# Moving the output projection's matmuls within the last batch of an attention kernel

## The reference

```python
def _L0_xattn_ref(query, key_value, Wq, bq, Wk, bk, Wv, bv, Wo, bo):
    ...
    scores = jnp.einsum('bhqd,bhkd->bhqk', Q, K) / scale
    weights = jax.nn.softmax(scores, axis=-1)
    attn = jnp.einsum('bhqk,bhkd->bhqd', weights, V)
    attn = attn.transpose(0, 2, 1, 3).reshape(B, SQ, H * Dh)
    return attn @ Wo.T + bo
...
x = x + _L0_xattn_ref(_layernorm(x, axis=-1), ctx_1024, ...)
x = x + _L0_attn_ref(_layernorm(x, axis=-1), ...)
```

## Time and profile before

| | |
|---|---|
| median of 3 runs | 2019.91 us (2019.12 to 2020.32) |
| the profiled execution, its own time | 2021.62 us |
| its span in the trace | 2019.8 us |
| PE busy | 1936.8 us, 96% |
| DVE, POOL, ACT busy | 1424.1 us (71%), 1263.3 us (63%), 895.7 us (44%) |
| last batch, first score maximum to the last shift | 1059.0 to 1182.5 us |
| mean granted PE clock, whole span | 0.983 |

### The profile page before, as it was taken

The page is one execution under the profiler, slowest core; times in us unless marked ns, Lnnn a source line. Parts: engine busy times, 40 slices in busy tenths (PEclk is TensorE's granted clock), DMA queues, the critical chain, the costliest instruction groups (busy, mean ns, idle before and its releaser), DMA issues. The chain is left out here.

```text
span 2019.8 us, 38857 instructions
## 1 busy us (share of the span) xinstructions
PE 1936.8 (96%) x15364; PEld 1416.2 (70%) x15364; DVE 1424.1 (71%) x1479; ACT 895.7 (44%) x1204; POOL 1263.3 (63%) x990
## 2 busy tenths in 40 slices
PE   6989999999999999999998889899999999999998
PEld 5867777777777777777774558555555555768886
DVE  4126777777777777677776856399999998538675
ACT  4124444434444344443433544476676664533340
POOL 4127777777777777777767731089989996325210
PEclk9999999999999999999997899999999999999999
DMA  5546565555555555655544320230040003111201
GB/s 199 158 135 178 157 192 160 177 181 170 183 161 172 168 181 166 181 154 187 175 133 142 111 66 1 51 78 1 1 125 1 1 1 101 42 43 63 92 13 42
DMA packets 180550, 229.31 MB, mean 114 GB/s; under 512 B 21489, under 2 KB 111921, under 8 KB 174225
## 3 DMA queue, kind: packets, MB, share of 16 engines
q1 hardware_dynamic: 180368, 226.82, 36.5%
HBM read 153.18 MB, written 73.56 MB: 112 GB/s over the span
## 5 line engine op out<-in xcount | busy, mean ns | idle before, releaser
L525 POOL TENSOR_TENSOR a_half<-a_pt 128x1024 f32<-128x1024 f32 x128 | 307.6, 2403 | 251.6 <-ACT a_pt L600 243.9
L600 ACT ACTIVATE a_pt<-a_shift 128x2048 f32<-128x2048 f32 x128 | 245.1, 1915 | 471.8 <-PE a_o L903 455.4
L705 DVE TENSOR_TENSOR a_shift<-a_s,a_neg_rows 128x2048 f32<-128x2048 f32 x113 | 259.1, 2293 | 92.4 <-ACT a_neg_rows L611 92.4
L692 DVE TENSOR_REDUCE a_top<-a_s 128x128 f32<-128x2048 f32 x113 | 259.0, 2292 | 40.0 <-PE a_s L860 40.0
L819 PE MATMUL a_pj<-l_x_hi,l_w_hi 128*128 128x512 f32 x448 | 208.0, 464 | 0.0
L516 POOL TENSOR_TENSOR l_x_lo<-a_raw,l_x_hi 128x512 fp32r<-128x512 f32 x120 | 156.1, 1301 | 80.8 <-ACT l_x_hi L587 80.8
L1300 POOL TENSOR_TENSOR s_even_drive<-s_du,l_rows 128x512 f32<-128x512 f32 x128 | 163.0, 1274 | 61.6 <-DMA s_c_row<-bc_scratch 59.8
L1308 POOL TENSOR_TENSOR s_odd_seen<-s_odd_state,s_c_row 128x512 f32<-128x512 f32 x128 | 162.5, 1270 | 34.9 <-DVE s_odd_state L1439 15.2
L1500 PEld LDWEIGHTS s_ps<-s_diag,s_du_t 128*128 128x128 f32 x1024 | 135.8, 194 | 62.3 <-issue 62.3
L821 PE MATMUL a_pj<-l_x_lo,l_w_hi 128*128 128x512 f32 x448 | 177.1, 395 | 0.0
L820 PE MATMUL a_pj<-l_x_hi,l_w_lo 128*128 128x512 f32 x448 | 177.1, 395 | 0.0
(11 more groups left out here) (274 smaller groups left out, 4054.2 us busy)
## 6 DMA issues: line engine op xcount, KB each, us to landing
kv_scratch<-a_k_new SPq DMA_DIRECT2D x128, 256.0 KB, 2.5
kv_scratch<-a_v_new SPq DMA_DIRECT2D x128, 256.0 KB, 3.5
a_stack<-kv_scratch SPq DMA_DIRECT2D x512, 64.0 KB, 2.4
a_v<-kv_scratch SPq DMA_DIRECT2D x32, 1024.0 KB, 6.2
a_raw<-in_ctx SPq DMA_DIRECT2D x120, 256.0 KB, 3.7
a_q_stack<-q_scratch SPq DMA_DIRECT2D x128, 64.0 KB, 2.1
s_c_row<-bc_scratch SPq DMA_DIRECT2D x32, 256.0 KB, 5.8
e_ew_raw<-in_ew SPq DMA_DIRECT2D x8, 1024.0 KB, 4.9
```

Source lines behind the costliest of these rows:

```text
L525: nc.gpsimd.tensor_tensor(half[:], w[:, 0:2], w[:, 2:4], ALU.add).then_inc(halved, 1)
L600: nc.scalar.activation(pt_head(g, p), shift[:].rearrange("p (i n) -> p i n", n=BANK), ACT.Exp).then_inc(exped, 1)
L692: dve.tensor_reduce(top[:], s_ps[:].rearrange("p i n -> p (i n)").rearrange("p (k q) -> p q k", q=L), AX.X, ALU.max).then_inc(blocked, 1)
L705: dve.tensor_tensor(shift[:].rearrange("p (k q) -> p k q", q=L), s_ps[:].rearrange("p i n -> p (i n)").rearrange("p (k q) -> p k q", q=L), ...
```

## The change

In the last batch's loop over heads, on PE alone, the seven-fold sequence of chunks 0 to 3 gets other places. Before, chunk 0 stood behind the weighing of an odd head, chunk 1 between the two turns of the next even head, chunk 2 behind that head's weighing, chunk 3 behind the second turn of the next odd head. Now chunk 0 stands between the turns of an even head, chunk 1 behind its second turn, chunk 2 between the turns of the next odd head and chunk 3 where it was. `turn_normalised` moves from behind the first turn to ahead of it. The number of instructions is the same on every engine; on DVE, ACT, POOL and SP the order is the same too.

```diff
             for h in range(1, H):
                 for s in range(2):
                     half_scores(h, s)
+                turn_normalised(h)
                 turn_half(h, 0)
-                turn_normalised(h)
+                project_output(h, 2, (0,))
+                project_output(h, 3, (2,))
+                turn_half(h, 1)
                 project_output(h, 2, (1,))
-                turn_half(h, 1)
                 project_output(h, 3, (3,))
                 spread_negative(LAST + h, 2)
                 weigh_last(B - 1, h // HG, h % HG, False)
-                project_output(h, 2, (2,))
-                project_output(h, 1, (0,))
```

## The result

| | before | after |
|---|---|---|
| median of 6 runs | 2020.12 us (2019.12 to 2022.2) | 2012.12 us (2011.88 to 2013.31) |
| ratio after / before, 95% interval | | 0.9968 (0.9956 to 0.998) |
| profiled execution: own time, span | 2021.62, 2019.8 us | 2011.88, 2010.1 us |
| first maximum of head 1 to the last head's shift | 121.17 us | 110.70 us |

The change makes the kernel faster, by 8.0 us between the medians. The interval of the ratio puts it between 4 and 9 us. The prediction was 2010.0 us in a range of 2004.5 to 2017.5. The profiled execution of the kernel before lies 1.5 us above its median, so the difference between the two traces (9.7 us of span) is somewhat larger than that between the medians.

The account below looks back on a forecast made before the run. The prediction took DVE to hold most of the pace, idle 17.6 us before next heads' maxima. Terms 3.1 + 6.8 + 1.0 - 1.0 + 0 gave 9.9 us off 2019.9: 2010.0 us, range 2004.5 to 2017.5.

Parts of the forecast that it names:

- the ring: DVE and PE handovers, with an ACT copy, from one head's first maximum to the next; DVE has most of it.
- The sum of 9.9 us: Total of the gains and prices in the last batch, against the profiled execution; taken from the 2019.9 us median.
- head 1 to 2: Scores of head 2 start 3.1 us earlier, without chunk 0 and its wait for DMAs.
- heads 2, 4, 8, 12: Even heads at the low clock lose the chunk behind the weighing: 4 x 1.7 = 6.8 us won.
- heads 6, 10, 14: Even heads at full clock: 0.5 us won before the next maximum, 0.17 paid ahead of the spread; 1.0 us together.
- transposes: turn_normalised ahead of the first turn in heads 7, 9, 11, 13, 15 costs 0.2 us each, 1.0 together.
- heads 3 and 5: Odd heads partly at the low clock: gain 0, bounds -0.85 and +0.9 us each.
- the lower bound of 1.0: Least gain per head in heads 2, 4, 8, 12, priced at the low clock throughout: 2.0 - 1.0 us.
- the price of the two chunks in the turns: In even heads a chunk ahead of the spread costs 0.17 us at full clock, about 1.0 at the low clock.
- The clock is back by the scores: In heads 2, 4, 8, 12 dense work from the first turn restores the clock; another 0.9 us per head goes.
- the clock hardly falls: Rival for the last batch: nearly all DVE waits go and low-clock costs come back, 15.8 us, 2004 us; chance 0.09.
- a sign against it: The low clock in heads 6, 7, 10, 11, 14 or 15 of the profile after would show the prediction wrong.

Follow-up runs that it names:

- the seventh experiment: Changed kernel plus six unread matmuls ahead of the first turn of heads 4, 8 and 12; 2006.53 us, ratio 0.9955 to the kernel before.
- the fifth experiment: Changed kernel with both chunks of heads 4, 8, 12 one place earlier, chunk 0 ahead of the first turn; 2008.72 us, ratio 0.996 to before.
- the third experiment: Changed kernel with chunk 0 left behind the weighing of odd heads and only chunk 1 between an even head's turns; 2015.58 us, ratio 0.9984 to before.
- ninth: Changed kernel plus unread matmuls: six ahead of the first turn of heads 4, 8, 12, three ahead of and three between head 1's turns; 2007.04 us.
- tenth: Kernel with one chunk in even heads plus unread matmuls: three and three in head 1, two behind chunk 0 in heads 4, 8, 12; 2006.92 us.
- eleventh: Changed kernel plus ten transposes of 128x128 ahead of the first turn of heads 4, 8 and 12; 2007.44 us, ratio 0.9951 to before.

## Why the prediction was right

The time came within 2.1 us of 2010.0, and the mechanism, chunks off the ring where DVE waits plus an earlier return of the clock, was the right one. The sum of 9.9 us agrees with the trace's last batch (10.5 us), but by terms that cancel, which is luck. By the table above, before minus after:

| term of the sum | predicted | in the traces |
|---|---|---|
| head 1 to 2 | 3.1 | 3.4 |
| heads 2, 4, 8, 12 | 6.8 | 2.27 + 0.23 + 1.79 + 1.40 = 5.7 |
| heads 6, 10, 14 | 1.0 | 0.19 - 1.05 + 0.16 = -0.7 |
| transposes | -1.0 | 0 to -0.1 |
| heads 3 and 5 | 0 | 0.96 + 1.17 = 2.1 |

**Head 1 to 2.** Right. The weighing ended earlier too, since it had the full clock for part of its time (1.25 against 1.94 us). PE then waited 0.53 us for half 0 of the shift.

**Even heads at the low clock.** The mean was 1.4 instead of 1.7, but head 4 won 0.23 us, far under the lower bound of 1.0. The step that was mis-sized is the price of the two chunks in the turns. The sum took the turns of these heads as at the low clock already. Those of heads 4 and 8 were not:

```profile
1090.29 0.33 PE L879 MATMUL a_m<-l_ident,a_top 128*128 128x128 f32 x1 [1.26 <-DVE a_top L712]
1090.45 1.02 PE L974 MATMUL a_pj<-l_wo,a_v_new 128*128 128x512 f32 x2
...
1092.27 0.32 PE L886 MATMUL a_m<-l_ident,a_neg_max 128*128 128x128 f32 x1 [0.52 <-DVE a_neg_max L718]
```

In head 4 first turn to spread took 1.98 us before and 3.69 us after (1083.01 to 1086.70, shown at the seventh experiment): 1.7 us more, which ate nearly all of the wait of 2.10 us that went. In head 8 it was 2.09 us before and 3.24 us after (1113.16 to 1116.40). "The clock is back by the scores" was right, and saved the term: in all four the scores ran at the full clock, in 2.29 us with the wait for half 1 in them. The fall itself I took as given. It still costs heads 4, 8 and 12 from 1.2 to 1.5 us each: filled, they take 6.60 us instead of 7.83 to 8.14. The case "the clock hardly falls" was priced at 16 us. With the three waits filled the last batch won 121.2 - 108.3 = 12.9, with heads 5 and 13 still falling (3.0 us over 7.11 and 7.13), so its size was about right, but the change alone did not reach it. Its argument that PE's wait would grow from 1.66 to about 2.1 us did not hold: it stayed at 1.66 to 1.67, since PE now waits for the shift ahead of the scores too.

**Full-clock even heads.** Mis-sized from 0.33 to 0.18 each. I let DVE go from the shift straight into the next maximum. In fact shift to next maximum is 2.57 us (1101.01 to 1103.58), with a wait of 0.21 us in every even head: half 0 of the shift, the handover and half of the scores do not quite fit into the shift. And head 10 fell to the low clock, 1.05 us slower than before, which the prediction had named as a sign against it. The stretch ahead of it has no long wait but several short ones: 0.88 us for the shift, a gap between the halves of the scores, 0.47 us for the maximum. PE's chunk behind the weighing had covered the first of them before. But heads 6 and 14 have the same waits (0.89 and 0.47 us) and kept the full clock, so they do not explain the fall by themselves.

**Transposes.** Mis-sized: 0.2 us per head predicted, nothing measured. The first turn comes 0.24 us later, as predicted (1103.58 to 1105.10 is 1.52 instead of 1.28 us), but the second turn waits for the second half's maximum in any case, and the turns move closer (0.97 instead of 1.13 us).

**Heads 3 and 5.** I left their gain at 0 with 0.9 as a bound. Both ran at the full clock after, head 5 in 7.11 instead of 8.28 us. Their 2.1 us hide what the even heads 2, 4, 8, 12 and head 10 won less.

**Behind the last batch** not all moved forward. First mixer matmul minus last head's shift was 1193.83 - 1180.20 = 13.6 us before and 1183.56 - 1169.12 = 14.4 after, and the rest of the kernel took 0.6 us longer. With 0.6 us that the last batch began earlier: 0.6 + 10.5 - 0.8 - 0.6 = 9.7, the difference of the spans.

**What is shown and what is argued.** That the clock at heads 4, 8 and 12 depends on whether PE has something to do ahead of the first turn is shown. In all eight kernels that put something into that place these heads took 6.5 to 6.8 us (only head 8 of the fifth experiment 7.07, with a fall at its end), with work that nobody needs as well as with chunks, and in the kernel before as in the changed one. In the six kernels that leave the place empty the clock fell at 16 of 18 such heads. The two exceptions are heads 8 and 12 of the third experiment, the second with the full wait of 1.66 us. So the wait is what makes a fall likely, and not a sufficient cause of it. Filling does not end all falls: in each of the eight filled kernels at least one of the heads right behind (5, 9 or 13) was at the low clock for a part, and in the changed kernel none of these three was.

That the scatter of the kernel before (10 us) comes from the clock is borne out by its 63 executions beside the experiments: the six fastest, 2011.29 to 2012.80 us, had mean granted clocks of 0.989 to 0.990, and the five above 2021 us 0.982 or 0.983. At which heads those executions fell is not on record, since each kernel has one trace. What decides whether a head with the long wait, or one with only short waits, falls stays open.

## What to carry to other kernels

Read a chain with PE in it at both clock levels before moving anything: at the low one a chunk of matmuls here cost 2.0 us instead of 1.05 and a fitting slot became a delay. Work that PE has to spare belongs where PE waits, and if there is none, a few unread matmuls in a wait of 1.7 us can pay (4.8 us of 2018 here for 18 of them, on the kernel before). Look at the heads behind as well: the fall may come there instead. A handover that waits on a DMA at the entry of a stage is worth its own look: one of 28 chunks carried 3.4 of the 10.5 us, less the 1.3 us that head 2 pays when only that chunk is moved.

## What had not been expected of the hardware

- The kernel before ran between 2011.29 and 2021.82 us in 26 runs; the kernel with the chunks in the turns within 1.4 us in six. The six runs of the kernel before beside those lay within 3.1 us, so that the order changed the scatter is not shown by so few.
- Adding 1.60 us of matmuls in three places made the kernel before faster by 4.8 us.
- Transposes held the full clock as well as matmuls did (heads 4, 8, 12 at 6.60 us with either).
- The same wait of 1.66 us ahead of head 12's first turn went with a fall of the clock in both kernels and with none in the third experiment.
- Without a long wait PE can still fall to the low clock: at head 10 of the changed kernel after waits of 0.88 and 0.47 us, while heads 6 and 14 with the same waits kept the full one.

The lowest times were those of the seventh, ninth, tenth and eleventh experiments, with unread work added (ratios 0.9948 to 0.9955, 2006.5 to 2007.4 us), and, without any useless work, that of the kernel with one chunk in even heads (0.9959, 2008.2 us). The intervals of all of them overlap each other and that of the changed kernel (0.9956 to 0.998), so by the times no order is claimed. In the traces the last batch of these kernels took 108.1 to 109.5 us against 110.7.
